# Layer 1 of a four-layer kernel: projections of split operands in three passes, a scan that works in place in three pairs of banks, and sums carried into the next round

## The chip, the core and the metric

The kernel runs on one core of a Trainium2 chip, in one launch. The metric is the device time of one execution in microseconds (us). Five engines run side by side and meet only at semaphores: PE (matrix products; "PEld" is its loading of weights), DVE (vector), ACT (scalar and table functions), POOL (general) and SP (issues most DMAs). PE writes to PSUM, eight banks of 512 fp32 values per partition; DVE and ACT read and write PSUM and SBUF; POOL here works on SBUF.

## What is computed

Four layers run one after the other on x of shape (8, 100, 512): a latent attention with an MLP, this case's layer 1, a cross attention with an MLP, and a grouped attention. Layer 1 is of the RWKV kind (the shift and the norms are cut here):

```
sx = shift(xa) - xa ;  t = tanh((xa + sx*maa_x) @ maa_w1)          # 5 groups of 32
xw, xk, xv, xr, xg = xa + sx*(maa_f + t_f @ maa_w2[f])               # the mixing
w = exp(-exp(time_decay + tanh(xw @ decay_w1) @ decay_w2))
r, k, v = xr @ Wr.T, xk @ Wk.T, xv @ Wv.T ;  g = silu(xg @ Wg.T)
def step(s, inp):                                                     # 32 heads of 16, over the 100 tokens
    a = k_l[..., :, None] * v_l[..., None, :]
    out = einsum('bhs,bhst->bht', r_l, faaaa * a + s)
    return a + w_l[..., None] * s, out
```

## The kernel before, in words

Features lie on the partitions: 512 features are KT = 4 tiles of 128, and the 800 columns of a tile are 8 batches of 100 tokens, cut into two halves of 400. Each stage is a block in which every engine runs its own written list; a barrier stands between blocks. Two stages matter.

`layer1_mixing` computes five branches f = w, k, v, r, g. For each, PE makes eight "mix" tiles (`project_features`, L1259), DVE turns each into sx*(maa_f + mix) (L1445), POOL adds xa (L1458, semaphore `completed`). The branch w then goes through two small decay products (`decay1`, `decay2`, with Tanh and twice Exp on ACT, L1394 to L1405). The other four are multiplied by a weight: PE transposes its 16 blocks (`turn_weight`, L1237), ACT and DVE copy them to SBUF (`copy_weight`), and PE multiplies in fp32 (L1259, `out_f`), ACT copying the results out (L1410). An fp32 matmul shows as two matmul rows in the trace. PE's order is mix_w, turn Wk, mix_k, decay, turn Wv, mix_v, out_k, turn Wr, mix_r, out_v, and so on: a weight is turned before the projection ahead of it. All of it moves through eight PSUM banks in rotation (`Tiles`): a tile waits until the tile eight before it is emptied.

`layer1_scan` goes through the four tiles in four rounds (a loop, m) of 16 steps t. For each step PE spreads row t of v of each head over the head's 16 partitions (a product with `spread[t]`, in the two parts `v.hi` and `v.lo` of a rounded fp32r value and its rest, L1597) into one PSUM pair `ps_v`; DVE multiplies by k into `ps_kv`, of which there are two pairs (L1551); ACT puts the starting state in column 0 of each batch (L1579); DVE runs the recurrence over 8 x 101 columns (`tensor_tensor_scan`, L1561); POOL multiplies by r (L1523), and four steps later (GATHER) PE adds it up in `ps_y` with `gather[t]` (L1607). DVE's order is product t, scan t-1, product t+1, scan t. PE's spreading of t waits for DVE's product t-1, which reads `ps_v`; DVE's product t waits for that spreading and for scan t-2. The last four sums of a round stand in PE's list ahead of the next round's first spreading, and ACT's copy of y (L1582) ends the round.

Lines that the prediction uses: the scan's two loops, and the one place where DVE's product waits:

```
dve.wait_ge(spreaded, at(m, N1, t))
dve.wait_ge(scanned, at(m, N1, t - 2))
```

`at(m, N1, t)` is the semaphore's count when event t of round m has happened.

Of the kernel before, what the change touches and what calls it, by code (L numbers as in the profile page):

```python
# [1262 lines left out]

def layer1_mixing(nc, k, ins, ctx, xa, T):

    with ExitStack() as own:
# [8 lines left out]
        mixed = [sb(f"mixed{i}", [P, KT, B * L]) for i in range(2)]  # L1275
# [8 lines left out]
        natural = [sb(f"W_natural{i}", [P, KT, D]) for i in range(2)]  # L1284
        turned = [sb(f"W_turned{i}", [P, KT, D]) for i in range(2)]
        stages = [("t", 4, "a")]
        for n in range(len(BRANCHES) + 1):
            if 1 <= n < len(BRANCHES):
                stages.append((f"W{BRANCHES[n]}", KT, "ad"))
            if n < len(BRANCHES):  # L1290
                stages.append((f"mix_{BRANCHES[n]}", 2 * KT, "d"))
            if n == 1:
                stages += [("decay1", HALVES, "a"), ("decay2", 2 * KT, "a")]
            elif n:
                stages.append((f"out_{BRANCHES[n - 1]}", 2 * KT, "a"))
        tiles = Tiles(k, "l1m", psum_banks(nc, own, "l1m_ps", 8), stages)
# [7 lines left out]
        completed = sem("l1m_completed")  # L1304
        exped = sem("l1m_exped")
# [3 lines left out]
        def _(sp):  # L1309
# [7 lines left out]
            for n, f in enumerate(BRANCHES[1:]):  # L1317
                if n >= 2:

                    tiles.wait_out(sp, f"W{BRANCHES[n - 1]}")  # L1320
                sp.dma_start(natural[n % 2][:], ins[f"L1_xattn_W{f}"].rearrange("(m p) i -> p m i", p=P)
                             ).then_inc(W_loaded[f], 16)

        @block.tensor
        def _(pe):
            pe.wait_ge(small, 16)

            for half in range(HALVES):
                for part in range(2):
                    j = 2 * half + part  # L1330
                    tiles.wait_free(pe, "t", j)
                    for t in range(KT):
                        if j == 0:
# [4 lines left out]
                                       half_tokens(mixed[0], t, half), start=(t == 0), stop=(t == KT - 1))  # L1338
                    mm.then_inc(tiles.filled, 1)
            def mix(n):  # L1340
                f = BRANCHES[n]
                if n:
                    turn_weight(pe, k, tiles, f"W{f}", natural[(n - 1) % 2], lambda: pe.wait_ge(W_loaded[f], 16))
                else:
                    tiles.wait_out(pe, "t")
                    pe.wait_ge(w2_loaded, 16 * 5)
# [7 lines left out]
            def project(n):  # L1354
                f, m_in = BRANCHES[n], mixed[(n + 1) % 2]
                pe.wait_ge(completed, 2 * KT * (n + 1))
                if f == "w":
                    pe.wait_ge(decay_loaded, 16 * 2)
                    for half in range(HALVES):
                        tiles.wait_free(pe, "decay1", half)  # L1360
                        for t in range(KT):
                            mm = pe.matmul(tiles.bank("decay1", half)[0:L_DECAY, 0:HALF], dw1[:, t, :],
                                           half_tokens(m_in, t, half), start=(t == 0), stop=(t == KT - 1))
# [4 lines left out]
                else:  # L1368
                    tiles.wait_out(pe, f"W{f}")
                    project_features(pe, tiles, f"out_{f}", lambda t, m: turned[(n - 1) % 2][:, t, m * P:(m + 1) * P],  # L1370
                                     lambda t, half: half_tokens(m_in, t, half), KT)

            for n in range(len(BRANCHES) + 1):
                if n < len(BRANCHES):
                    mix(n)
                if n:
                    project(n - 1)

        @block.scalar
        def _(act):  # L1380
            for half in range(HALVES):
                for part in range(2):
# [5 lines left out]
                                   ).then_inc(tiles.emptied["a"], 1)  # L1388
            def finish(n):
                f = BRANCHES[n]  # L1390
                if f == "w":
                    for half in range(HALVES):
# [3 lines left out]
                                       ).then_inc(tiles.emptied["a"], 1)  # L1396
                    for j in range(2 * KT):
# [15 lines left out]
            for n in range(1, len(BRANCHES) + 1):  # L1413
                if n < len(BRANCHES):
                    copy_weight(tiles, "a", act, f"W{BRANCHES[n]}", turned[(n - 1) % 2])
                finish(n - 1)

        @block.vector
        def _(dve):
# [5 lines left out]
            for t in range(KT):  # L1425
                dve.wait_ge(differed, t + 1)
                dve.scalar_tensor_tensor(by_batch(mixed[0][:, t, :]), by_batch(sx[:, t, :]),
                                         column(k, "L1_xattn_maa_x", t), xa[:, t, :, 1:PREV], ALU.mult, ALU.add
                                         ).then_inc(first_mixed, 1)
            for n, f in enumerate(BRANCHES):  # L1430
                if f != "w":
                    copy_weight(tiles, "d", dve, f"W{f}", turned[(n - 1) % 2])
                if n == 1:

                    tiles.wait_out(dve, "t")
                for j in range(2 * KT):
                    m, half = divmod(j, HALVES)
                    tiles.wait_filled(dve, f"mix_{f}", j)
                    if n >= 2 and j == 0:

                        back = BRANCHES[n - 2]
                        tiles.wait_filled(dve, "decay1" if back == "w" else f"out_{back}",
                                          (HALVES if back == "w" else 2 * KT) - 1)

                    dve.scalar_tensor_tensor(half_tokens(mixed[(n + 1) % 2], m, half),  # L1445
                                             tiles.bank(f"mix_{f}", j)[:, 0:HALF], column(k, f"L1_xattn_maa_{f}", m),
                                             half_tokens(sx, m, half), ALU.add, ALU.mult
                                             ).then_inc(tiles.emptied["d"], 1)

        @block.gpsimd  # L1450
        def _(pool):
            k.sems.clear_ended(pool)
            for n, f in enumerate(BRANCHES):
                for j in range(2 * KT):
                    m, half = divmod(j, HALVES)
                    tiles.wait_out(pool, f"mix_{f}", [j])
                    dst = by_batch(half_tokens(mixed[(n + 1) % 2], m, half))
# [3 lines left out]
def layer1_scan(nc, k, ins, ctx, T, yT, prefetch):  # L1461
# [6 lines left out]
    GATHER = 4  # L1468
    with ExitStack() as own:
# [10 lines left out]
        v = Split(own, nc, "v_split", [P, KT, B * L])  # L1480
# [5 lines left out]
        ps_v = own.enter_context(nc.psum_tensor("ps_v", [P, HALVES, 512], F32))  # L1486
        ps_kv = [own.enter_context(nc.psum_tensor(f"ps_kv{i}", [P, 1024], F32)) for i in range(2)]
# [4 lines left out]
        built = sem("l1s_built")  # L1492
        spreaded = sem("l1s_spread")
# [8 lines left out]
        v_split = sem("l1s_v_split")  # L1502
        block = own.enter_context(nc.Block())
# [10 lines left out]
        def _(pool):  # L1514
            k.sems.clear_ended(pool)
            pool.sem_inc(received, 2 * N1)
# [10 lines left out]
        def _(dve):  # L1527
# [5 lines left out]
            dve.tensor_reduce(k.head_of[:], ident, AX.X, ALU.add)  # L1533
            dve.memset(gather[:], 0.0).then_inc(built, 1)
# [3 lines left out]
            dve.wait_ge(built, 2)  # L1538
            for t in range(N1):
                dve.tensor_scalar(spread[:, t, :], k.same_head[:], rows[:, t:t + 1], None, ALU.mult)  # L1540
                last = dve.tensor_copy(gather[:, t, t:P:N1], k.same_head[:, t:P:N1])
            last.then_inc(built, 1)
            for t in range(KT):
                dve.wait_ge(v_rounded, t + 1)
                v.rest(dve, lambda x: x[:, t, :], T["v"][:, t, :]).then_inc(v_split, 1)
            with dve.Fori(0, KT) as m:
                for t in range(N1 + 1):
                    if t < N1:
                        dve.wait_ge(spreaded, at(m, N1, t))
                        dve.wait_ge(scanned, at(m, N1, t - 2))  # L1550
                        dve.tensor_tensor(  # L1551
                            kv[t % 2][:, :, 1:PREV].rearrange("p (h b) l -> p h b l", h=HALVES),
                            ps_v[:, :, 0:HALF].rearrange("p h (b l) -> p h b l", l=L),
                            T["k"][:, bass.ds(m, 1), :].squeeze(1).rearrange("p (h b l) -> p h b l", h=HALVES, l=L),
# [1972 lines left out]
```

## Time and profile before

| | us |
|---|---|
| three runs: median (lowest to highest) | 3405.37 (3399.28 to 3408.23) |
| the profiled execution, its own time | 3410.99 |
| its span, first to last instruction | 3408.9 |
| mixing stage of layer 1, 599.7 to 749.6 | 149.9 |
| scan stage of layer 1, 749.6 to 970.6 | 221.0 |
| PE busy over the whole span | 3079.6 (90%) |
| mean granted PE clock | 0.948 |

The stages follow one another, so what is changed in layer 1 is read from its two stages. In the rows below, times count from the span's start. A duration is that of one instruction with its fixed part; where instructions follow closely, the distance of their starts tells what one costs. "PEclk" is the clock that PE was granted as a share of 2.4 GHz.

### The profile page before, as it was taken

How to read it: one execution, taken by the hardware profiler on the slowest of the kernel's cores; microseconds unless marked ns; L12 is line 12 of the kernel's file. 1: busy time of each engine (PE TensorE's matmuls, PEld its weight loads, DVE VectorE, ACT ScalarE, POOL GpSimd, SP SyncE). 2: the span in 40 equal slices, each digit the busy share in tenths (PEclk: the TensorE clock that was granted, in tenths of full speed). 3: DMA queues.
4: the chain of work that ended last, by engine and by line, in shares of the span. 5: the costliest groups of instructions: out<-in, count | busy, mean ns of one | idle time of the engine just before them, and what ended most of it. 6: DMA issues, size and time to landing. Idle time of an engine off the chain costs nothing. (4 is left out here: it accounts for less than half of the span.)

```text
span 3408.9 us, 47898 instructions
## 1 busy us (share of the span) xinstructions
PE 3079.6 (90%) x17313; PEld 2567.3 (75%) x17313; DVE 1912.0 (56%) x3919; ACT 1470.1 (43%) x3387; POOL 863.1 (25%) x880
## 2 busy tenths in 40 slices
PE   5999898987778789999999988999999997989997
PEld 4777497544434589989999888998989986955663
DVE  2444533328863466665566666666566555147774
ACT  2444442220011244455544644446554464246771
POOL 0222400305541321132011431104101041055632
PEclk9999999988898899999999999999999998988997
DMA  4131020100001320114101241012401023021110
GB/s 125 65 98 40 26 75 6 56 16 0 0 0 37 98 80 27 46 53 130 52 27 46 71 145 45 28 45 76 132 27 53 20 82 102 1 75 39 58 23 20
DMA packets 131964, 182.75 MB, mean 54 GB/s; under 512 B 17743, under 2 KB 99548, under 8 KB 131740
## 3 DMA queue, kind: packets, MB, share of 16 engines
q1 hardware_dynamic: 119012, 143.96, 13.7%
q0 software_dynamic: 12544, 35.77, 3.4%
q8 instruction: 139, 2.28, 0.3%
q14 instruction: 85, 0.70, 0.1%
q10 hardware_dynamic: 184, 0.05, 0.0%
HBM read 165.88 MB, written 13.86 MB: 53 GB/s over the span
## 5 line engine op out<-in xcount | busy, mean ns | idle before, releaser
L71 PE MATMUL l2a<-l_arena,l_arena 128*128 128x400 f32 (+2 forms) x1856 | 652.1, 351 | 34.5 <-DVE l_arena L2724 14.7
L72 PE MATMUL l2a<-l_arena,l_arena 128*128 128x400 f32 (+2 forms) x1856 | 632.7, 341 | 0.0
L73 PE MATMUL l2a<-l_arena,l_arena 128*128 128x400 f32 (+2 forms) x1856 | 632.6, 341 | 0.0
L71 PEld LDWEIGHTS l2a<-l_arena,l_arena 128*128 128x128 f32 (+1 forms) x1856 | 352.4, 190 | 56.8 <-issue 47.0
L72 PEld LDWEIGHTS l2a<-l_arena,l_arena 128*128 128x128 f32 (+1 forms) x1856 | 354.0, 191 | 2.7
L73 PEld LDWEIGHTS l2a<-l_arena,l_arena 128*128 128x128 f32 (+1 forms) x1856 | 352.6, 190 | 2.0
L2589 ACT ACTIVATE l_arena<-l2a 121x384 fp32r<-121x384 f32 (+1 forms) x208 | 99.6, 479 | 442.5 <-PE l2a L2364 442.5
L2384 PE MATMUL l2a<-l_arena,l_arena 121*128 121x384 f32 (+1 forms) x768 | 279.4, 364 | 3.2 <-DVE l_arena L2790 3.2
L2386 PE MATMUL l2a<-l_arena,l_arena 121*128 121x384 f32 (+1 forms) x768 | 264.0, 344 | 0.0
L2385 PE MATMUL l2a<-l_arena,l_arena 121*128 121x384 f32 (+1 forms) x768 | 263.3, 343 | 0.0
L2239 POOL DMA_DIRECT2D p_dram_layer<-l_arena x128 | 62.7, 495 | 726.1 <-DVE l_arena L2790 724.4
L2768 DVE TENSOR_REDUCE neg_max_layer<-l2a 128x1 f32<-128x362 f32 (+1 forms) x208 | 110.8, 533 | 203.0 <-PE l2a L73 196.0
L3337 ACT ACTIVATE probs<-probs,neg_max 100x363 f32<-100x363 f32 x256 | 151.4, 595 | 92.6 <-DVE neg_max L3374 88.8
L3374 DVE CUSTOM_DVE_ANT_0 probs<-scores,mask 100x363 f32<-100x363 f32 x256 | 134.0, 532 | 81.5 <-PE scores L3285 76.0
L2813 DVE TENSOR_TENSOR l_arena<-Qp_layer,l_arena 128x400 fp32r<-128x400 f32 x256 | 155.9, 669 | 18.6 <-ACT l_arena L2630 18.0
L432 POOL TENSOR_SCALAR probs<-probs,inverse 100x464 f32<-100x464 f32 x128 | 83.6, 653 | 299.8 <-DVE inverse L636 299.7
L3293 PEld LDWEIGHTS turned<-ident,probs 100*121 100x121 f32 x768 | 127.5, 208 | 39.0 <-ACT probs L3337 25.9
L2756 DVE TENSOR_TENSOR l_arena<-Qp_layer,l_arena 128x512 fp32r<-128x512 f32 (+1 forms) x208 | 139.1, 671 | 29.7 <-ACT l_arena L2548 29.7
L3293 PE MATMUL turned<-ident,probs 100*121 100x100 f32 x768 | 137.0, 292 | 19.9 <-ACT probs L3337 13.3
L1523 POOL TENSOR_TENSOR rs<-r_tile,state 128x800 f32<-128x800 f32 x64 | 111.5, 1742 | 149.1 <-DVE state L1561 149.1
L2384 PEld LDWEIGHTS l2a<-l_arena,l_arena 121*128 121x128 f32 x768 | 144.6, 188 | 6.0 <-DVE l_arena L2790 3.8
L2790 DVE TENSOR_TENSOR l_arena<-l2a,l_arena 121x384 fp32r<-121x384 f32 (+1 forms) x208 | 112.7, 542 | 63.3 <-ACT l_arena L2589 63.3
(427 smaller groups left out, 6918.1 us busy)
## 6 DMA issues: line engine op xcount, KB each, us to landing
l_arena<-in_L_xattn_wq_dram SPq DMA_DIRECT2D x32, 512.0 KB, 3.5
l_arena<-in_L_xattn_wk_dram SPq DMA_DIRECT2D x32, 512.0 KB, 5.0
l_arena<-in_L_xattn_wv_dram SPq DMA_DIRECT2D x32, 512.0 KB, 3.5
l_arena<-in_L_xattn_wo_dram SPq DMA_DIRECT2D x64, 256.0 KB, 2.7
l_arena<-ctxT_hi POOLq DMA_DIRECT2D x16, 724.0 KB, 4.6
l_arena<-ctxT_lo POOLq DMA_DIRECT2D x16, 724.0 KB, 6.1
l0mlp_staged<-in_L_xattn_mlp_w_dram SPq DMA_DIRECT2D x16, 512.0 KB, 4.1
l2mlp_staged<-in_L_xattn_w_fc_dram SPq DMA_DIRECT2D x16, 512.0 KB, 4.2
```

The lines of the kernel that those rows point to most:

```text
L71: pe.matmul(out, cut_a(a.hi), cut_b(b.hi), start=start, stop=False)
L72: pe.matmul(out, cut_a(a.hi), cut_b(b.lo), start=False, stop=False)
L73: return pe.matmul(out, cut_a(a.lo), cut_b(b.hi), start=False, stop=stop)
L2384: pe.matmul(out, c_hi[s][0:T2, n, rows], probsT.hi[0:T2, n, ring], start=(n == 0), stop=False)
L2385: pe.matmul(out, c_hi[s][0:T2, n, rows], probsT.lo[0:T2, n, ring], start=False, stop=False)
L2386: mm = pe.matmul(out, c_lo[s][0:T2, n, rows], probsT.hi[0:T2, n, ring], start=False, stop=(n == NT2 - 1))
L2756: dve.tensor_tensor(Qt[i % 2].lo[:, :, 0:n], Qp[:, :, c, rows], Qt[i % 2].hi[:, :, 0:n].bitcast(F32), ALU.subtract).then_inc(qt_lo, 1)
L2790: dve.tensor_tensor(probsT.lo[0:T2, :, cols], ps_t[i % 2][0:T2, 0:NT2 * P].rearrange("p (n l) -> p n l", l=P)[:, :, 0:n], probsT.hi[0:T2, ...
L2813: dve.tensor_tensor(u[h % 2].lo[:, t, :].rearrange("p (b q) -> p b q", q=L), head_columns(Qp, h)[:, t], u[h % 2].hi[:, t, :].bitcast(F32). ...
L3293: mm = pe.transpose(ps_turned[h % 2][0:T3, j * L:(j + 1) * L], probs[h % PROBS][:, j * T3:(j + 1) * T3], k.ident[0:L, 0:L])
L3337: act.activation(probs[h % PROBS][:], probs[h % PROBS][:], ACT.Exp, bias=neg_max[:, h % H3:h % H3 + 1], scale=-1.0).then_inc(exped, 1)
L3374: dve.tensor_tensor_reduce(probs[h % PROBS][:], ps_scores[h % SCORES][0:L, 0:N3], mask_add[b % 2][:], -1.0, 3e38, ALU.add, ALU.min, neg_ma ...
```

## The change

In the mixing, the four weighted projections use operands split in two fp32r parts, a rounded one (`hi`, written by ACT) and the rest (`lo`, by DVE): three products hi*hi, hi*lo, lo*hi (`product`, L69) take the place of the fp32 one. Whole values now lie in `T["g"]` (in `T["r"]` for branch w). The split needs ACT to round eight half tiles of each branch and DVE to subtract them, three tiles behind its mixing (REST_BEHIND), and ACT to round and DVE to subtract each turned weight in place of the copies. There is one buffer for a loaded weight and one for a turned one, so PE now turns a weight after the projection ahead of it, and SP loads the next weight once the last is turned. In the scan, PE spreads v into the very pair of banks in which DVE multiplies in place and scans, three pairs in turn; v has a zero column per batch, so 808 columns go in pieces of 512 and 296. The last four sums of a round and the copy of y are carried into the next round (the first round sums zeros, y gets one tile more); part of the building of `spread` goes to ACT, that of `gather` and some zeros to POOL.

PE's list at the start of the mixing, up to the first projection, before (names: `t_four` and `t_decay` are tanh results, `W_natural` the loaded weight, `l1m_ps` the banks):

```order
L1259 MATMUL l1m_ps<-t_four,maa_w 128x400 x8
L1237 MATMUL l1m_ps<-ident,W_natural 128x128 x16
L1259 MATMUL l1m_ps<-t_four,maa_w 128x400 x8
L1362 MATMUL l1m_ps<-mixed,decay_w 64x400 x8
L1259 MATMUL l1m_ps<-t_decay,decay_w 128x400 x8
L1237 MATMUL l1m_ps<-ident,W_natural 128x128 x16
L1259 MATMUL l1m_ps<-t_four,maa_w 128x400 x8
L1259 MATMUL l1m_ps<-mixed,W_turned 128x400 x32
```

and now:

```order
L1259 MATMUL l1m_ps<-t_four,maa_w 128x400 x16
L1366 MATMUL l1m_ps<-T_r,decay_w 64x400 x8
L1259 MATMUL l1m_ps<-t_decay,decay_w 128x400 x8
L1237 MATMUL l1m_ps<-ident,W_natural 128x128 x16
L1259 MATMUL l1m_ps<-t_four,maa_w 128x400 x8
L71 MATMUL l1m_ps<-mixed_hi,W_turned_hi 128x400
L72 MATMUL l1m_ps<-mixed_lo,W_turned_hi 128x400
L73 MATMUL l1m_ps<-mixed_hi,W_turned_lo 128x400
```

One turned weight less stands ahead of the first projection, and the weight it needs is turned behind the decay products.

DVE's list at the end of a round of the scan, before:

```order
L1551 TENSOR_TENSOR ps_kv<-ps_v,T_k 128x8x100 [waits l1s_scanned,l1s_spread]
L1561 SCALAR_TENSOR_TENSOR state<-T_w,ps_kv 128x808 [waits l1s_received,l1s_started,l1s_keyed]
L1549 REGISTER_ALU
L1551 TENSOR_TENSOR ps_kv<-ps_v,T_k 128x8x100 [waits l1s_scanned,l1s_spread]
L1561 SCALAR_TENSOR_TENSOR state<-T_w,ps_kv 128x808 [waits l1s_received,l1s_started,l1s_keyed] x2
```

and now:

```order
L1604 TENSOR_TENSOR ps_kv<-ps_kv,T_k 128x8x100 [waits l1s_spread]
L1611 SCALAR_TENSOR_TENSOR state<-T_w,ps_kv 128x808 [waits l1s_received,l1s_started,l1s_keyed]
L1602 REGISTER_ALU
L1604 TENSOR_TENSOR ps_kv<-ps_kv,T_k 128x8x100 [waits l1s_spread]
L1611 SCALAR_TENSOR_TENSOR state<-T_w,ps_kv 128x808 [waits l1s_received,l1s_started,l1s_keyed] x2
```

The order of DVE is the same; the product no longer waits for a scan. That wait is now PE's, ahead of its spreading.

PE's list at the end of a round, before:

```order
L1597 MATMUL ps_v<-v_split_hi,spread 128x400 x2
L1597 MATMUL ps_v<-v_split_lo,spread 128x400 x2
L1607 MATMUL ps_y<-rs,gather 128x400 x8
L1603 REGISTER_ALU
L1607 MATMUL ps_y<-rs,gather 128x400 x2
L1591 REGISTER_ALU
L1591 COMPARE_AND_BRANCH
```

and now:

```order
L1677 MATMUL ps_kv<-v_split_hi,spread 128x512
L1677 MATMUL ps_kv<-v_split_hi,spread 128x296
L1677 MATMUL ps_kv<-v_split_lo,spread 128x512
L1677 MATMUL ps_kv<-v_split_lo,spread 128x296
L1666 MATMUL ps_y<-rs,gather 128x400 x2
L1671 REGISTER_ALU
L1671 COMPARE_AND_BRANCH
L1666 MATMUL ps_y<-rs,gather 128x400 x8
```

The last four sums of a round no longer stand between its last spreading and the branch; the eight behind the branch are those of the last round.

The diff, cut to its core:

```diff
+REST_BEHIND = 3
 def layer1_mixing(nc, k, ins, ctx, xa, T):
+        whole = [T["r"]] + [T["g"]] * (len(BRANCHES) - 1)
+        mixed = [Split(own, nc, f"mixed{i}", [P, KT, B * L]) for i in range(2)]
+        natural = sb("W_natural", [P, KT, D])
+        turned = Split(own, nc, "W_turned", [P, KT, D])
...
         @block.tensor
             for n in range(len(BRANCHES) + 1):
                 if n < len(BRANCHES):
                     mix(n)
                 if n:
                     project(n - 1)
+                if 1 <= n < len(BRANCHES):
+                    turn_weight(pe, k, tiles, f"W{BRANCHES[n]}", natural,
+                                lambda: pe.wait_ge(W_loaded[BRANCHES[n]], 16))
...
         @block.scalar
+            def round_mixed(n, tiles_of):
+                for j in tiles_of:
+                    m, half = divmod(j, HALVES)
+                    act.wait_ge(completed, 2 * KT * n + j + 1)
+                    mixed[n % 2].round(act, lambda x: half_tokens(x, m, half), half_tokens(whole[n], m, half)
+                                       ).then_inc(mix_rounded, 1)
+            def round_weight(n):
+                for t in range(KT):
+                    tiles.wait_filled(act, f"W{BRANCHES[n]}", t)
+                    turned.round(act, lambda x: x[:, t, :], tiles.bank(f"W{BRANCHES[n]}", t)[:]).then_inc(W_rounded, 1)
             def finish(n):
                 if f == "w":
+                    round_mixed(1, range(KT))
...                  # the two Tanh
+                    round_mixed(1, range(KT, 2 * KT))
...                  # the sixteen Exp
                 else:
                     for j in range(2 * KT):
+                        if n + 1 < len(BRANCHES) and j < KT:
+                            round_mixed(n + 1, (2 * j, 2 * j + 1))
...
+            for n in range(len(BRANCHES)):
+                finish(n)
+                if n + 1 < len(BRANCHES):
+                    round_weight(n + 1)
...
 def layer1_scan(nc, k, ins, ctx, T, y_and_one, prefetch):
+    BANKS = [0, 1, 2] * 5 + [1]
+    PIECES = (slice(0, 512), slice(512, B * PREV))
+    def last_in_banks(t):
+        return max(u for u in range(t - N1, t) if BANKS[u % N1] == BANKS[t])
...
         @block.gpsimd
+            pool.memset(gather[:], 0.0).then_inc(blank, 1)
+            for t in range(N1):
+                last = pool.tensor_copy(gather[:, t, t:P:N1], k.same_head[:, t:P:N1])
+            for tile in rs:
+                last = pool.memset(tile[:], 0.0)
...
         @block.vector
-                        dve.wait_ge(scanned, at(m, N1, t - 2))
-                        dve.tensor_tensor(
-                            kv[t % 2][:, :, 1:PREV].rearrange("p (h b) l -> p h b l", h=HALVES),
-                            ps_v[:, :, 0:HALF].rearrange("p h (b l) -> p h b l", l=L),
+                        spread_v = kv[BANKS[t]][:, :, 1:PREV]
+                        dve.tensor_tensor(spread_v, spread_v, by_batch(T["k"][:, bass.ds(m, 1), :].squeeze(1)),
+                                          ALU.mult).then_inc(keyed, 1)
...
         @block.tensor
+            for half in range(HALVES):
+                pe.matmul(ps_y[:, half, 0:HALF], gather[:, 0, :], rs[0][:, half * 4:(half + 1) * 4, :], start=True, stop=False)
             with pe.Fori(0, KT) as m:
+                for t in range(N1):
+                    pe.wait_ge(scanned, at(m, N1, last_in_banks(t)))
+                    for part in (v.hi, v.lo):
+                        flat = part[:].rearrange("p m b l -> p m (b l)")
+                        for piece in PIECES:
+                            mm = pe.matmul(ps_kv[BANKS[t]][:, piece], spread[:, t, :],
+                                           flat[:, bass.ds(m, 1), piece].squeeze(1),
+                                           start=(part is v.hi), stop=(part is v.lo))
+                    mm.then_inc(spreaded, 1)
+                    gather_heads(m, t - GATHER)
+            for t in range(GATHER):
+                gather_heads(KT, t - GATHER)
```

## Rows read from the trace of the kernel before

**Rows 1.** Windows, layer 1's mixing and scan: us, length, busy (instructions), PEclk, DMA, GB/s.
```profile
599.70:749.60 149.90, 147.59 (x464) 81.52 (x464) 33.55 (x51) 34.34 (x64) 36.97 (x40) 0.97 0.08 28
749.60:970.60 221.00, 164.82 (x512) 100.35 (x513) 185.50 (x168) 21.59 (x76) 111.47 (x64) 0.88 0.03 6
```

**Rows 2.** Waits 749 to 971 us: who waited for whom, us in total, times, longest.
```profile
DVE ps_kv L1551 <- PE ps_v L1597: 24.9, 12, 4.4
```

**Rows 3.** Timeline, one settled scan step: start, us, engine, line, out<-in, count [idle, releaser].
```profile
783.98 1.00 DVE L1551 TENSOR_TENSOR ps_kv<-ps_v,T_k 128x800 f32<-128x800 f32 x1
784.89 1.83 DVE L1561 TENSOR_TENSOR_SCAN state<-T_w,ps_kv 128x808 f32<-128x808 f32 x1
...
785.87 1.50 PE L1607 MATMUL ps_y<-rs,gather 128*128 128x400 f32 x4
...
786.82 1.00 DVE L1551 TENSOR_TENSOR ps_kv<-ps_v,T_k 128x800 f32<-128x800 f32 x1
```

**Rows 4.** Timeline of DVE, from the scan's first round to its second.
```profile
807.59 3.56 DVE L1561 TENSOR_TENSOR_SCAN state<-T_w,ps_kv 128x808 f32<-128x808 f32 x2
...
815.59 1.00 DVE L1551 TENSOR_TENSOR ps_kv<-ps_v,T_k 128x800 f32<-128x800 f32 x1 [4.45 <-PE ps_v L1597]
...
817.68 1.00 DVE L1551 TENSOR_TENSOR ps_kv<-ps_v,T_k 128x800 f32<-128x800 f32 x1 [1.09 <-PE ps_v L1597]
```

**Rows 5.** Timeline of PE, mixing.
```profile
619.63 1.91 PE L1237 MATMUL l1m_ps<-ident,W_natural 128*128 128x128 f32 x16
...
674.74 21.66 PE L1259 MATMUL l1m_ps<-mixed,W_turned 128*128 128x400 f32 x64
...
703.64 44.92 PE L1259 MATMUL l1m_ps<-mixed,W_turned 128*128 128x400 f32 x128
```

**Rows 6.** Timeline of PE in layer 2, split products of 400 columns.
```profile
1902.95 0.34 PE L71 MATMUL l2a<-l_arena,l_arena 128*128 128x400 f32 x1
...
1904.40 0.34 PE L73 MATMUL l2a<-l_arena,l_arena 128*128 128x400 f32 x1
```

**Rows 7.** Timeline of POOL, ACT and PE around the decay projections.
```profile
615.85 14.77 POOL L1458 TENSOR_TENSOR mixed<-mixed,xa 128x400 f32<-128x400 f32 x16 [28.39 <-DVE mixed L1445]
...
632.98 1.28 ACT L1402 ACT_TABLE_LOAD   x1
...
634.28 0.59 ACT L1402 ACTIVATE T_w<-l1m_ps,params 128x400 f32<-128x400 f32 x1
...
642.70 1.07 ACT L1245 ACTIVATE W_turned<-l1m_ps 128x512 f32<-128x512 f32 x2
...
646.13 6.21 PE L1259 MATMUL l1m_ps<-mixed,W_turned 128*128 128x400 f32 x18
```

**Rows 8.** DMA issues in the mixing: count, KB each, us from issue to landing.
```profile
W_natural<-in_L_xattn_Wv_dram SPq DMA_DIRECT2D x1, 1024.0 KB, 8.0
```

**Rows 9.** DVE's groups by form: out<-in, shapes, count, busy, mean ns, idle before.
```profile
L58 DVE TENSOR_TENSOR l0mlp_gT_lo<-l0mlp_g,l0mlp_gT_hi 128x400 fp32r<-128x400 f32 x32 | 18.4, 575 | 89.7 <-ACT l0mlp_gT_hi L54 89.7
...
L58 DVE TENSOR_TENSOR l_hT_lo<-l_whole,l_hT_hi 128x400 fp32r<-128x400 f32 x8 | 5.4, 743 | 0.0
```

**Rows 10.** Timeline of PE, its first product of the scan stage.
```profile
761.09 1.03 PE L1597 MATMUL ps_v<-v_split_hi,spread 128*128 x2 [12.52 <-DVE v_split_lo L58]
```

**Rows 11.** POOL's groups by form.
```profile
L3091 POOL MEMSET values<- 121x768 f32 x2 | 1.5, 737 | 154.4 <-POOLq L949 154.4
...
L866 POOL COPY xa<-states 128x32 f32<-128x32 f32 x1 | 0.2, 235 | 0.0
```

**Rows 12.** Windows of PE: us, length, busy (instructions), PEclk, DMA, GB/s.
```profile
774.00:778.00 4.00, 4.00 (x9) 0.50 0.00 0
...
790.00:806.00 16.00, 12.99 (x46) 1.00 0.00 1
```

**Rows 13.** Timeline of DVE, the first settled product, and the last two scans.
```profile
778.30 1.00 DVE L1551 TENSOR_TENSOR ps_kv<-ps_v,T_k 128x800 f32<-128x800 f32 x1 [1.22 <-PE ps_v L1597]
...
962.32 3.55 DVE L1561 TENSOR_TENSOR_SCAN state<-T_w,ps_kv 128x808 f32<-128x808 f32 x2
```

More of the change, by code:

```diff
@@ L1362, in project @@
                             mm = pe.matmul(tiles.bank("decay1", half)[0:L_DECAY, 0:HALF], dw1[:, t, :],
-                                           half_tokens(m_in, t, half), start=(t == 0), stop=(t == KT - 1))
+                                           half_tokens(whole[0], t, half), start=(t == 0), stop=(t == KT - 1))
                         mm.then_inc(tiles.filled, 1)
@@ L1368, in project @@
                 else:
+                    pe.wait_ge(mix_split, 2 * KT * n)
                     tiles.wait_out(pe, f"W{f}")
-                    project_features(pe, tiles, f"out_{f}", lambda t, m: turned[(n - 1) % 2][:, t, m * P:(m + 1) * P],
-                                     lambda t, half: half_tokens(m_in, t, half), KT)
+                    for j in range(2 * KT):
+                        m, half = divmod(j, HALVES)
+                        tiles.wait_free(pe, f"out_{f}", j)
+                        for t in range(KT):
+                            mm = product(pe, tiles.bank(f"out_{f}", j)[:, 0:HALF], turned, m_in,
+                                         lambda x: x[:, t, m * P:(m + 1) * P], lambda x: half_tokens(x, t, half),
+                                         start=(t == 0), stop=(t == KT - 1))
+                        mm.then_inc(tiles.filled, 1)
             for n in range(len(BRANCHES) + 1):
@@ L1430, in _ @@
             for n, f in enumerate(BRANCHES):
-                if f != "w":
-                    copy_weight(tiles, "d", dve, f"W{f}", turned[(n - 1) % 2])
                 if n == 1:
                     tiles.wait_out(dve, "t")
[L1436 to L1448, printed above, removed]
+                for j in range(2 * KT + (REST_BEHIND if n else 0)):
+                    if j < 2 * KT:
+                        m, half = divmod(j, HALVES)
+                        tiles.wait_filled(dve, f"mix_{f}", j)
+                        dve.scalar_tensor_tensor(half_tokens(whole[n], m, half), tiles.bank(f"mix_{f}", j)[:, 0:HALF],
+                                                 column(k, f"L1_xattn_maa_{f}", m), half_tokens(sx, m, half),
+                                                 ALU.add, ALU.mult).then_inc(tiles.emptied["d"], 1)
+                    if n and j >= REST_BEHIND:
+                        split_mixed(n, j - REST_BEHIND)
@@ L1450, in _ @@
+                if n:
+                    for t in range(KT):
+                        dve.wait_ge(W_rounded, KT * (n - 1) + t + 1)
+                        turned.rest(dve, lambda x: x[:, t, :], tiles.bank(f"W{f}", t)[:]).then_inc(tiles.emptied["d"], 1)
         @block.gpsimd
@@ L1537, in _ @@
                             k.head_of[:].unsqueeze(2).broadcast_to([P, P // N1, N1])).then_inc(built, 1)
[L1538 to L1542, printed above, removed]
             for t in range(KT):
                 dve.wait_ge(v_rounded, t + 1)
-                v.rest(dve, lambda x: x[:, t, :], T["v"][:, t, :]).then_inc(v_split, 1)
+                v.rest(dve, lambda x: x[:, t, :, 1:PREV], by_batch(T["v"][:, t, :])).then_inc(v_split, 1)
+            dve.wait_ge(built, 2)
+            for t in range(0, N1, 2):
+                last = dve.tensor_scalar(spread[:, t, :], k.same_head[:], rows[:, t:t + 1], None, ALU.mult)
+            last.then_inc(spread_dve, 1)
             with dve.Fori(0, KT) as m:
@@ L1587, in _ @@
             pe.sem_inc(spreaded, 2 * N1)
[L1588 to L1589 removed]
+            pe.sem_inc(gathered, 2 * N1 - GATHER)
             pe.wait_ge(v_split, KT)
[L1591 to L1610 removed]
```

132 lines of the change are left out of this document (72 added, 60 removed).

## The prediction

> **What bounds the kernel now.** I read the windows by stage first, since the diff touches two stages of layer 1 only. The mixing takes 149.9 us with PE busy for 147.6 of them: there PE's own work sets the time. The scan takes 221.0 us with PE busy for 164.8, DVE for 185.5 and POOL for 111.5 [rows 1]: nobody fills it. The waits say who is late there: DVE stood 24.9 us before its product, in 12 waits of up to 4.4 us, for PE's spreading of v [rows 2]. The timelines show the two kinds of it. A settled step is 2.84 us from product to product (783.98 to 786.82): the product lasts 1.00, the scan starts 0.91 after it and lasts 1.83, and the next product starts 0.10 after the scan's end [rows 3]. So inside a round DVE is the bound. Between rounds it isn't: the last two scans end at 811.15, the next product starts at 815.59 and the one after it 2.09 later [rows 4], since the next spreading stands behind the last four sums in PE's list and behind DVE's product in turn.
>
> **The mixing.** Four projections of 32 products each, 128 in all. An fp32 product is two rows of the trace; 64 of them take 21.66 us, 0.338 each [rows 5], 0.677 a product. The split form stands in layer 2: from 1902.95 to 1904.40 eight of them start, 0.181 each [rows 6], 0.544 for three. 128 x 0.133 = 17.0 us gained.
>
> Against it stand three losses. First, the path to the first projection. One turned weight (1.9 us [rows 5]) leaves PE's list ahead of the decay products, so these come 1.9 earlier; but ACT must now round four half tiles between the second Tanh and its table load. POOL's adds come every 0.92 (14.77/16); w's are done at 623.2, and k's follow DVE, which puts rests between its products, to about 630.7. The second Tanh ends by 631.1 (632.98 less 1.9), four roundings at no more than 0.535 (two copies of 512 in 1.07) end at 633.2, the table load of 1.28 at 634.5: the first Exp is 0.2 later than 634.28. The sixteen Exps take as long as before, 8.42 (634.28 to 642.70). ACT's four roundings of Wk end at 645.1, DVE's last rest at 646.3, and mix_v's last four tiles need exactly those banks, so PE ends mix_v at 647.0 and starts out_k there, against 646.13 [rows 7]: 0.9 lost. Second, one turned weight more now lies behind that point: 1.9. Third, Wg is turned last, with nothing of PE's behind it: ACT's copy of the last tile and four roundings, then DVE's last rest, end some 4.0 us after out_r, PE's transposes 1.9 after: 2.1 of waiting. Wv and Wr have a mix (5.5 us) to hide in. SP now issues the next weight's load when the last one is turned; the load (8.0 us [rows 8]) has a projection and a mix, 23 us, to hide in, and nothing of this stage stands behind it in SP's queue. The new work of DVE (32 rests of 0.575 [rows 9], and subtractions of weights in place of copies) and of ACT (32 roundings and 8 more of weights) comes to some 20 us each, on top of 33.6 and 34.3 in a stage of 150 [rows 1]; behind out_k it lies beside PE's projections and costs nothing. The dip behind 703.64, where 128 rows take 44.92 and not twice 21.66 [rows 5], follows the same 32-row mix in both and stays.
>
> DVE's rests and POOL's adds both read two tiles of SBUF. A rest of 400 columns takes 0.575 where POOL rests, and 0.743 on average in the one group that ran beside POOL's adds [rows 9]. If the four rests of k held up POOL for their whole length, 4 x 0.575 less the 0.4 of slack (631.1 less 630.7) would be lost, 1.9; by the means of the rows it is 4 x 0.168 less the slack, 0.3. I take 0.5, near the rows, with 0 and 1.9 as ends. The Trainium skill (SBUF — State Buffer, "Who interferes with whom") says that a DVE instruction with two SBUF inputs and a GpSimd one that reads SBUF lock each other out for their whole length. By that rule the loss is the upper end, 1.9, and the mixing's gain 1.4 smaller; the rows agree that they disturb each other, not that each rest does so in full.
>
> Mixing: 17.0 - 0.9 - 1.9 - 2.1 - 0.5 = 11.6 us less.
>
> **The scan's start.** Its first spreading starts at 761.09 [rows 10], 11.5 after the stage [rows 1]. DVE is relieved of zeros, 16 small copies and 8 of its 16 `spread` tiles; POOL takes the zeros and the copies, and new zeros for `rs`. POOL's price by the nearest rows: 768 columns of zeros cost 0.737, a copy of 32 columns 0.235 [rows 11]. 2048 columns are 2.0, 16 copies at most 3.8 (2.4 if they overlap by a third), four times 800 columns 3.1: 7.5 to 9, behind the clearing of semaphores that opens POOL's list and that no row shows; I add 1, and up to 3 more where POOL and DVE disturb each other. PE then starts 11 (8.5 to 13) after the stage. It first sums zeros, four matmul rows at half clock (0.50 [rows 12], so twice 0.338 each), 2.7; the spreading of step 0 takes 1616 columns at 1.2 GHz, 1.35; then come sums of zeros again and the spreading of step 1. If the clock rises behind the first spreading these take 1.35 and 0.73, if it doesn't 2.7 and 1.35; with some 0.4 until DVE starts, the second product stands 17.5 to 19.5 after the stage, and I take 18.1, since PE now works without a break where before it waited until 774. Before, the first settled product, the sixth, stands at 778.30 [rows 13], which puts the second at 17.4 by steps of 2.84. 0.7 lost; with PE's start at 8.5 and a risen clock 2.4 would be gained, at 13 and half clock 4.1 lost.
>
> **The scan's steps.** With three pairs PE spreads up to three steps ahead, and DVE's product no longer waits for the scan before it, which is what left the 0.10 after each scan. Where two DVE instructions follow without such a wait, the second starts before the first ends: the scan 0.09 before the product's end [rows 3], two scans in 3.56 and not 3.66 [rows 4]. So a step becomes 0.91 + 1.73 = 2.64, if the product behind the scan does likewise; the bounds are 2.64 and 2.84. I take 2.64, as both neighbours show it.
>
> Two waits are left in a round. Step 15 shares its pair with step 13, so its spreading starts when scan 13 ends: DVE waits 1.09, as at 817.68 [rows 4], instead of overlapping by 0.10: 1.19. Step 1 of the next round shares with step 15: DVE does product 0 meanwhile (0.91) and stands at 1.09 after the last scan. From product 1 to the end of scan 15: 14 x 2.64 + 1.19 + 0.91 + 3.56 = 42.6; a further round 1.09 + 42.6 = 43.7. Four rounds: 42.6 + 3 x 43.7 = 173.7. Before, from the second product (767.0 by the step above) to 965.87, the end of the last scan [rows 13]: 198.9. Gain 25.2.
>
> What is queued behind the new waits: PE's wait for a scan holds back the sum behind it, which POOL's `rs` buffers of four steps need; POOL (111.5 us over 64 steps, 1.74 each [rows 1]) has them early, since its step is shorter than DVE's. ACT's copy of y, now between steps 3 and 4, delays the column of step 4 by 0.84, which has a step and a half of slack. PE's work of a step is 1616 columns of spreading, 0.73, and four rows of sums, 1.35 by their pace (1.50 with the last one's tail [rows 3]), together 2.08 of 2.64. The tail behind the last scan is unchanged.
>
> Scan: 25.2 - 0.7 = 24.5 less. Together 36.1 less: 3411.0 of the profiled execution become 3374.9. That execution lies 5.6 over the median shown, so against the median 3405.4 it is 3369.
>
> **Rivals.**
> - *No overlap behind the scan.* The step stays at 2.84: four rounds take some 184, the gain of the scan's steps is 14.8, the time 3380. For it: no row shows a product starting behind a scan that it doesn't wait for; against it: both other orders overlap. The Trainium skill (VectorE: DVE Perf Modes, "The DRAIN you can't avoid") says that the next instruction doesn't issue until the pipe is empty, with a semaphore or without; by it this rival would be the forecast. The overlapped starts of [rows 3, 4] speak against it, or make the drain shorter than the rule has it.
> - *In place is slow.* Every DVE row before writes another bank than it reads, or SBUF. If reading and writing one bank take turns, 800 elements cost 0.85 more (1.00 for 800 [rows 3] against 0.575 for 400 [rows 9], twice the difference), 64 times, 54 us: 3423. It decides against the change from 0.56 us a product on. No row excludes it, and none points to it.
> - *PE at half clock.* A step would cost 1.35 + 2.7 = 4.0 on PE, above DVE's 2.64, 64 of them 257 instead of 199: about 3450. Against it: 12.99 busy of 16 us kept the clock at 1.00 [rows 12], and PE's share now is 78% a step without the pauses between rounds.
> - *The mixing pays less.* ACT, POOL and DVE hold up more than I count (1.9 for the locks, the clock after PE's wait for Wg), and the start takes its worst: 1.4, some 1.6 and 3.4 more, 3376.
> - *The start pays*, and no lock costs: 3.6 more gained, 3365.
>
> **How the numbers follow.** The forecast 0.52, with a range of its own from 3361 to 3377; no overlap 0.18; mixing and start worse 0.12; start better 0.08; in place slow 0.07; half clock 0.03. 3357 to 3386 holds the first four and leaves the last two and odd ends out. 0.3%, 10 us, is about what a measurement here can tell. Faster by more: 0.89, the first four less a little; slower 0.08, the last two less a part-priced slow product; within 0.03.
>
> **What would show it.** Split rows at a pace of 0.181 in the mixing and PE waiting about 2 us ahead of out_g; a step of 2.64 with products of 1.00; a wait of about 1.1 at step 15 of each round and none of 4.4; PE's clock at 1.00 from the third step on. A product far over 1.00, a step of 2.84, or a PE that DVE waits for in most steps would make it wrong.

## The result and the profile after

The changed kernel took 3368.4 us (median of four runs, 3366.0 to 3379.6) against 3405.2 for the kernel before beside it (four runs, 3399.3 to 3408.2): a ratio of 0.9901, 95% interval 0.9882 to 0.9919. Two more comparisons, on two different chips, gave 0.9907 (0.9870 to 0.9943) and 0.9905 (0.9888 to 0.9921). 3369 was forecast.

The profiled execution took 3379.6, the slowest of its four; that of the kernel before, 3411.0, lay above all its other runs too. The two spans differ by 31.1 (3408.9 and 3377.8) and the medians by 36.8. The windows of after by stage answer to [rows 1, 12]; below them are a projection, the stretch behind the 32-row mix, the scan's start, and the first spreadings of step 15 in rounds 1 and 4 (columns as there, PEclk third from the end):

```profile
core 0: us, PE busy (x) PEld busy (x) DVE busy (x) ACT busy (x) POOL busy (x), PEclk, DMA share, GB/s
599.53:740.18 140.65, 134.54 (x592) 104.69 (x592) 59.63 (x91) 53.12 (x104) 42.87 (x40) 0.96 0.09 30
740.18:931.87 191.69, 155.62 (x524) 92.59 (x524) 175.01 (x143) 23.65 (x84) 118.89 (x86) 0.95 0.03 7
...
646.94:664.78 17.84, 17.84 (x99) 17.65 (x98) 10.01 (x15) 7.51 (x15) 9.38 (x8) 1.00 0.00 1
697.26:703.00 5.74, 5.74 (x17) 5.69 (x18) 1.09 (x3) 1.35 (x3) 2.77 (x3) 0.50 0.00 0
752.30:754.30 2.00, 2.00 (x7) 1.47 (x6) 0.00 (x0) 0.00 (x0) 0.00 (x0) 0.50 0.00 0
754.30:757.00 2.70, 2.70 (x11) 1.84 (x11) 1.36 (x2) 0.99 (x2) 0.00 (x0) 0.98 0.00 0
793.50:794.60 1.10, 1.05 (x5) 0.94 (x6) 0.01 (x1) 0.00 (x0) 1.02 (x1) 1.00 0.00 0
925.65:927.40 1.75, 1.75 (x5) 1.56 (x6) 0.00 (x1) 0.00 (x0) 1.73 (x1) 0.50 0.00 0
```

The mixing went from 149.9 to 140.65, the scan up to the end of the last scan from 216.3 (749.60 to 965.87, [rows 13]) to 191.69: 9.2 and 24.6, together 33.8. PE, which filled the mixing before, now waits in it. DVE's waits of the scan, answering to [rows 2] (waiter, waited for: us in total, times, longest):

```profile
DVE ps_kv L1604 <- PE ps_kv L1677: 16.6, 9, 8.3
```

8.3 of the 16.6 is the wait ahead of the first product. What is left is in the timeline of DVE: a settled step [rows 3], step 15 and the boundary of the first round [rows 4], and the same of the second:

```profile
775.04 0.97 DVE L1604 TENSOR_TENSOR ps_kv<-ps_kv,T_k 128x800 f32<-128x800 f32 x1
775.92 1.83 DVE L1611 TENSOR_TENSOR_SCAN state<-T_w,ps_kv 128x808 f32<-128x808 f32 x1
777.66 0.97 DVE L1604 TENSOR_TENSOR ps_kv<-ps_kv,T_k 128x800 f32<-128x800 f32 x1
...
794.59 1.00 DVE L1604 TENSOR_TENSOR ps_kv<-ps_kv,T_k 128x800 f32<-128x800 f32 x1 [1.09 <-PE ps_kv L1677]
795.50 3.55 DVE L1611 TENSOR_TENSOR_SCAN state<-T_w,ps_kv 128x808 f32<-128x808 f32 x2
798.97 0.97 DVE L1604 TENSOR_TENSOR ps_kv<-ps_kv,T_k 128x800 f32<-128x800 f32 x1
800.14 1.00 DVE L1604 TENSOR_TENSOR ps_kv<-ps_kv,T_k 128x800 f32<-128x800 f32 x1 [0.20 <-PE ps_kv L1677]
...
838.81 1.00 DVE L1604 TENSOR_TENSOR ps_kv<-ps_kv,T_k 128x800 f32<-128x800 f32 x1 [1.81 <-PE ps_kv L1677]
839.72 3.55 DVE L1611 TENSOR_TENSOR_SCAN state<-T_w,ps_kv 128x808 f32<-128x808 f32 x2
843.19 0.97 DVE L1604 TENSOR_TENSOR ps_kv<-ps_kv,T_k 128x800 f32<-128x800 f32 x1
845.21 1.00 DVE L1604 TENSOR_TENSOR ps_kv<-ps_kv,T_k 128x800 f32<-128x800 f32 x1 [1.04 <-PE ps_kv L1677]
```

A step is 2.62 (775.04 to 777.66), and the product starts at 777.66, 0.09 before the scan's end at 777.75. The boundary of 4.45 and 2.09 is gone. Step 15 waits 1.1 in rounds 1 and 3, but 1.81 in rounds 2 and 4; PE's timeline shows why (behind the 32-row mix and the wait for Wg, answering to [rows 5], then the scan's start and the spreadings of step 15 in rounds 1 and 4):

```profile
691.26 6.00 PE L1259 MATMUL l1m_ps<-t_last,maa_w_last 32*128 32x400 f32 x16
697.19 0.70 PE L71 MATMUL l1m_ps<-mixed_hi,W_turned_hi 128*128 128x400 f32 x1
697.69 0.54 PE L72 MATMUL l1m_ps<-mixed_lo,W_turned_hi 128*128 128x400 f32 x1
...
717.54 1.91 PE L1237 MATMUL l1m_ps<-ident,W_natural 128*128 128x128 f32 x16
721.39 0.42 PE L71 MATMUL l1m_ps<-mixed_hi,W_turned_hi 128*128 128x400 f32 x1 [1.94 <-issue]
...
750.14 3.00 PE L1657 MATMUL ps_y<-rs,gather 128*128 128x400 f32 x4 [11.00 <-POOL rs L1569]
...
793.55 0.63 PE L1677 MATMUL ps_kv<-v_split_hi,spread 128*128 x2 [2.91 <-DVE state L1611]
...
925.65 1.04 PE L1677 MATMUL ps_kv<-v_split_hi,spread 128*128 x2 [2.90 <-DVE state L1611]
```

PE stands 2.9 us for scan 13 in every round. At 793.55 it comes back at a granted clock of 1.00 (2.4 GHz), at 925.65 at 0.50 (1.2 GHz): the same two matmuls take 0.63 and 1.04.

### The profile page after: what moved, and what is told of

Its sections match the earlier page's. It is cut to its first block and busy times, and to the rows that moved or that the text cites. A ratio compares the mean times of both kernels' runs of the same rounds, so it can differ in the third digit from the quotient of the medians.

```text
span 3377.8 us, 48217 instructions
## 1 busy us (share of the span) xinstructions
PE 3059.4 (91%) x17461; PEld 2582.4 (76%) x17461; DVE 1934.5 (57%) x3934; ACT 1493.1 (44%) x3436; POOL 879.2 (26%) x903
## 5 line engine op out<-in xcount | busy, mean ns | idle before, releaser
L2458 PEld LDWEIGHTS l2a<-l_arena,l_arena 121*128 121x128 f32 x768 | 144.5, 188 | 6.0 <-DVE l_arena L2864 3.8
L2459 PEld LDWEIGHTS l2a<-l_arena,l_arena 121*128 121x128 f32 x768 | 145.0, 189 | 2.2
```

The source lines that it names most:

```text
L2458: pe.matmul(out, c_hi[s][0:T2, n, rows], probsT.hi[0:T2, n, ring], start=(n == 0), stop=False)
L2459: pe.matmul(out, c_hi[s][0:T2, n, rows], probsT.lo[0:T2, n, ring], start=False, stop=False)
```

## The experiments

Stage lengths by windows, the scan up to the end of its last scan; the ratio is to the kernel before beside it:

| kernel | mixing | scan | median us | ratio (95%) |
|---|---|---|---|---|
| before | 149.89 | 216.27 | 3405.2 | |
| after, three traces | 140.65, 139.78, 139.80 | 191.69, 191.86, 191.89 | 3368.4, 3373.0, 3368.3 | 0.9901, 0.9907, 0.9905 |
| mixing alone | 139.76 | 215.77 | 3393.4 | 0.9984 (0.9969-0.9999) |
| scan alone | 149.87 | 191.77 | 3380.5 | 0.9945 (0.9926-0.9965) |
| wait for the scan put back | 139.90 | 206.17 | 3388.3 | 0.9960 (0.9943-0.9977) |
| sums kept in the round | 139.58 | 202.30 | 3373.9 | 0.9919 (0.9900-0.9938) |
| pairs in threes throughout | 139.67 | 183.96 | 3370.5 | 0.9885 (0.9851-0.9920) |
| and no sums of zeros | 139.89 | 176.69 | 3355.9 | 0.9856 (0.9822-0.9890) |
| fifth mix over 128 rows | 136.18 | 191.83 | 3364.1 | 0.9883 (0.9846-0.9920) |
| the last three edits together | 136.41 | 176.66 | 3352.4 | 0.9851 (0.9833-0.9870) |

**Each half alone.** The mixing of after with the scan of before, and the other way round.

> Only the mixing is changed; the scan is that of the kernel before. Theory (the two halves of the change are independent, and the mixing pays its measured 9.2 us: 140.65 for the stage in the trace of after, 149.89 in that of before): about 3396, the mixing stage 140 to 141.5, the scan stage 216 to 217 as before. Rival (what the mixing gains is partly handed back behind it, as the 2.9 us by which the trace of after is longer than that of before between the last scan and the end would have it): 3399 or more with a mixing stage of 140.65 all the same.

> Only the scan is changed; the mixing is that of the kernel before. Theory: the scan pays its 24.6 us (191.7 in place of 216.3) whatever stands ahead of it: about 3381, steps of 2.62 to 2.63. Rival (the scan's start, or TensorE's clock in it, hangs on the split products ahead of it): a scan stage 2 us or more away from 191.7. If the theories of this run and of the mixing alone both hold, the two gains come to 33.8 of the 36.8 us of the medians.

Both stages came out as in after (10.1 and 24.5 less than before): the halves are independent. In total time the mixing alone gave 0.3 to 10.5 us by its interval, too wide to tell its theory from its rival. By the medians (before beside them: 3402.8) the two halves gave 9.4 and 22.3.

**Part of the time is not the change's.**

> The changed kernel again, on the chip and beside the runs that the next three are compared with. By the traces so far the mixing stage takes 139.6 to 140.7 and the scan 191.7; what lies behind the last scan, which no edit touches, took from 2437 to 2450 us in six traces, so a single execution is uncertain by that much. Theory: 33 to 37 less than before on the same chip.

It came out 34 less by the medians, 32 by the ratio. From the last scan to layer 2's last product the changed kernel takes 1849.9 us in the profile above and 1850.7 in a third trace of the same kernel; from there to the end, first in the one, then in the other:

```profile
2781.80:3377.80 596.00, 514.03 (x3057) 377.27 (x3056) 336.97 (x947) 293.97 (x576) 211.95 (x144) 0.89 0.15 46
```
```profile
2780.30:3369.40 589.10, 510.58 (x3057) 377.84 (x3056) 333.23 (x947) 293.97 (x576) 212.16 (x144) 0.89 0.15 46
```

596.0 and 589.1: with the same instructions, layer 3 alone differs by 7. So a stage is compared by its own length, and single executions are not. The totals of the next two runs miss what was expected of them by as much, one up and one down (3388 for 3380, 3374 for 3381).

**The wait that went.**

```
 dve.wait_ge(spreaded, at(m, N1, t))
+dve.wait_ge(scanned, at(m, N1, t - 2))
```

> After, with one wait put back: VectorE's product waits for the end of the scan ahead of it in VectorE's own list. Theory (the step fell from 2.84 to 2.63 because that wait is gone, the third pair and in place only make it possible): a settled step of 2.82 to 2.84, 56 steps of 64 by 0.21, so 11.8 us: about 3380. Rival (the product would start 0.09 before the scan's end in any case, since it is VectorE that lets the next instruction in early, and the 0.20 came from PE being ahead): step 2.63, 3368.

DVE's timeline of it, a settled step:

```profile
773.35 1.00 DVE L1605 TENSOR_TENSOR ps_kv<-ps_kv,T_k 128x800 f32<-128x800 f32 x1
774.26 1.83 DVE L1612 TENSOR_TENSOR_SCAN state<-T_w,ps_kv 128x808 f32<-128x808 f32 x1
776.19 1.00 DVE L1605 TENSOR_TENSOR ps_kv<-ps_kv,T_k 128x800 f32<-128x800 f32 x1
```

2.84, the product 0.10 behind the scan's end at 776.09: the step of the kernel before, from this one wait, with three pairs and in place. The rival is refuted. The scan lost 14.5, not 11.8. The settled steps are 52 and not 56, 13 a round, since DVE waits for PE at step 15 either way: 11.2 by 0.215. Step 15 now waited 1.81 in all four rounds and the second product behind each boundary 1.0, in the trace of after only in two rounds and at one boundary: 3.0 more. The rest is the start.

**The sums carried over.**

```
...                                   # ACT's copy of y likewise
-    gather_heads(m, t - GATHER)
-for t in range(GATHER):
-    gather_heads(KT, t - GATHER)
+    if t >= GATHER:
+        gather_heads(m, t - GATHER)
+for t in range(N1 - GATHER, N1):     # inside the round
+    gather_heads(m, t)
```

> After, with the last four sums and the copy of y back at the end of their round, three pairs and in place kept; the first sum of zeros is left out, POOL's zeros are not. Theory (the carrying is what takes away the 4.4 us at each round's end): the last scan is followed by POOL's product, the sums and the next spreading, so VectorE stands about 4.4 us and the product after that 2.1 later, 6.5 in place of 1.1 to 1.9, three times: 15 lost; the start without sums of zeros gains 2 to 3; about 3381. Rival (three pairs alone would do, the next round's spreadings start during the last scans): boundaries of 1 to 2 us, 3366.

The first boundary, DVE's timeline:

```profile
789.52 3.56 DVE L1611 TENSOR_TENSOR_SCAN state<-T_w,ps_kv 128x808 f32<-128x808 f32 x2
797.86 1.90 DVE L1604 TENSOR_TENSOR ps_kv<-ps_kv,T_k 128x800 f32<-128x800 f32 x2 [4.79 <-PE ps_kv L1673]
```

The 4.4 to 4.8 are back, so carrying the sums and the copy is what removed them; but the second product follows the first at once (1.90 for two), since with three pairs PE spreads several steps in a row. The expected 2.1 behind it did not come, and the scan lost 10.6 where 12 to 13 were expected (15 at the boundaries less the start).

**The waits that stayed.** The loop over rounds written out, step t of all 64 in pair t modulo 3:

```
-BANKS = [0, 1, 2] * 5 + [1]
+def pair(m, t):
+    return (N1 * m + t) % 3
-with pe.Fori(0, KT) as m:            # and dve, act, pool
+for m in range(KT):
-pe.wait_ge(scanned, at(m, N1, last_in_banks(t)))
+pe.wait_ge(scanned, at(m, N1, t - 3))
```

> After, with the loop over the four rounds written out, so that the pairs of banks go round in threes over all 64 steps and no two steps two apart share a pair. Theory (step 15's wait of 1.1 to 1.8 and the 1.1 to 1.9 behind each round's last scan come from the shared pair alone, and the larger of each pair of numbers from a spreading at TensorE's half clock after TensorE stood 2.9 us for scan 13): from the second product on DVE has 62 steps of 2.625 without a wait, then 4.44 to the end, 167.2 in place of 175.2: scan stage 183.7, 8 us less than after. Rival (code written out four times has to be fetched, or POOL's product and the sums hold PE at the old places): waits of over 0.5 remain once per 16 steps, gain under 4 us.

DVE's waits in its whole scan:

```profile
DVE ps_kv L1603 <- PE ps_kv L1676: 9.6, 2, 8.2
```

Two waits, ahead of the first two products, and none behind. The scan took 183.96 (183.7 expected), PE's clock was 1.00 from the fourth step to its end. The shared pair made those waits: the loop was written out in the same run, but in the trace of after it is DVE's scan that PE waits for at step 15 (2.91 at 793.55).

**The start.** That, and without the sums of zeros, POOL's zeros for them, and PE's wait for `gather` moved to its first use:

```
-pe.wait_ge(gather_built, 1)
-pe.wait_ge(rs_blank, 1)
-for half in range(HALVES):
-    pe.matmul(ps_y[:, half, 0:HALF], gather[:, 0, :], rs[0][...], start=True, stop=False)
+    if m > 0 or t >= GATHER:
+        gather_heads(m, t - GATHER)
```

> The one before, and the sums of zeros ahead of the first step and in steps 0 to 3 are left out, with POOL's zeros for them. Theory (the first spreading waits for POOL's list, which ends with those zeros at 750.0, 3.7 behind VectorE's and ScalarE's parts, and then for TensorE's sums of zeros at half clock, 2.2): the first product starts 8.5 us after the mixing and not 14.5, the second 10.5 and not 16.5: scan stage 177.5 to 178.5, 6 less than with cyclic pairs alone. Rival (TensorE stays at its lower clock longer without those sums, so that the first steps cost 3.8 in place of 2.6): 2 to 4 of the 6 are lost again.

PE's first spreadings, and DVE's first products:

```profile
746.11 1.01 PE L1668 MATMUL ps_kv<-v_split_hi,spread 128*128 128x512 f32 x2 [7.42 <-DVE spread L1592]
...
751.96 1.04 PE L1668 MATMUL ps_kv<-v_split_hi,spread 128*128 128x512 f32 x2 [1.48 <-DVE state L1606]
```
```profile
747.83 1.00 DVE L1599 TENSOR_TENSOR ps_kv<-ps_kv,T_k 128x800 f32<-128x800 f32 x1 [1.93 <-PE ps_kv L1668]
749.17 1.00 DVE L1599 TENSOR_TENSOR ps_kv<-ps_kv,T_k 128x800 f32<-128x800 f32 x1 [0.35 <-PE ps_kv L1668]
```

The products start 8.1 and 9.4 after the mixing (739.73), 7.3 gained on the kernel above. PE does stay at half clock longer, as the rival has it (1.04 at 751.96), but DVE waits no more behind the second product, so that costs nothing: PE is ahead by then.

**The fifth mix over 128 rows.** `t_last` and `maa_w_last` get 96 rows of zeros.

```
-w2_last = sb("maa_w2_last", [F_MIX, D])
+w2_last = sb("maa_w2_last", [P, D])
-t_last = sb("t_last", [F_MIX, B * L])
+t_last = sb("t_last", [P, B * L])
```

> After, with the fifth mix multiplied over 128 rows, 96 of them zeros, in place of 32. In after the products behind it run at a granted clock of 0.50 for 5.6 us (697.3 to 703.0), which makes that projection 20.35 long and the others 17.84. Theory (it is the 32-row products that make the clock fall): no fall, out_r 17.85, mixing stage 138, 2.5 less. Rival (the clock falls for another reason, such as the turning and mixing by themselves, which before Wv's projection it doesn't): the same fall, mixing 140 to 141.

```profile
687.81 5.54 PE L1259 MATMUL l1m_ps<-t_last,maa_w_last 128*128 128x400 f32 x16
692.88 0.66 PE L71 MATMUL l1m_ps<-mixed_hi,W_turned_hi 128*128 128x400 f32 x1
693.38 0.35 PE L72 MATMUL l1m_ps<-mixed_lo,W_turned_hi 128*128 128x400 f32 x1
```

PE's timeline at the same place: the second product takes 0.35 where it took 0.54, and the clock doesn't fall. The mixing is 3.6 less than in the trace of after beside it, more than the 2.5 expected, because that trace has two falls of the clock and the profile of after only one, a longer one. The second comes 1.0 behind the start of out_g, which PE starts after its wait of 1.94 for Wg. The two falls in the trace of after beside it, then out_g of this run (columns as in [rows 1]):

```profile
695.60:698.80 3.20, 3.20 (x11) 3.20 (x11) 0.76 (x2) 0.00 (x0) 2.88 (x3) 0.50 0.00 0
719.50:722.60 3.10, 3.10 (x11) 3.10 (x11) 0.00 (x0) 0.50 (x1) 0.00 (x0) 0.50 0.00 0
```
```profile
714.55:732.30 17.75, 17.75 (x96) 17.43 (x96) 0.00 (x0) 3.69 (x8) 0.00 (x0) 1.00 0.00 0
```

The padded mix takes both away: out_r takes 17.82 for 19.17, out_g with what follows it in the stage 18.80 for 20.32, the mix 5.07 for 5.57 from start to start; that is 3.4 of the 3.6. Seven traces of the new mixing with the 32-row mix have both falls, the profiled one has the first alone, and the two with the padded mix have none. Why the second goes with the first is not shown.

**All three together.**

> After with the three edits together: pairs of banks going round in threes over all 64 steps, no sums of zeros, the fifth mix over 128 rows. Theory (they lie in stages of their own and add up): mixing 136.2, scan 176.7, so 18.7 less than the 331.6 that the two stages of after took beside these runs: some 19 us less than after, ratio to before 0.984 to 0.986. Rival (the later layers, whose time differs by up to 12 us between executions though nothing in them is changed, swallow part of it): stages as said, ratio above 0.987.

> After beside it, on the same chip: ratio to before 0.989 to 0.992, mixing 139.6 to 140.7, scan 191.7 to 191.9.

The stages add up (313.1 against 331.7). 3352.4 against 3368.3 beside it, ratios of 0.9851 (0.9833 to 0.9870) and 0.9905 (0.9888 to 0.9921), which don't overlap: this version beats the changed kernel too, by 15.9 in the medians and 18.6 in the stages. After beside it came out as expected.

## Why the prediction was right

36.1 was forecast against its own profiled execution; the two stages gave 33.8 to 34.5, the three ratios 32 to 34. The forecast's mechanism held and no rival came whole; but a part of one did, terms of the mixing were off both ways, and two errors in the scan cancelled.

*Mixing: 11.6 forecast, 9.2 to 10.1 measured.* The 9.2 is of the profiled execution, which is not the usual one: the nine other traces with the new mixing agree with one another up to out_k, and the seven of them with the 32-row mix to the end of the stage. Term by term, from the second trace of after (10.1):

- The pace of 0.181 was nearly right (0.183), the 17.0 made of it too large: a projection of 96 rows takes 17.84 and not 17.4, since its second row starts 0.49 behind the first. That is 1.7 over four.
- "The dip ... stays" was right: out_r takes 1.3 more than the others (19.17 for 17.83); before, the dip cost 1.6 [rows 5]. But the sum put at nothing the second fall of the clock, behind PE's wait for Wg: 1.5. The prediction had it among its rivals ("the mixing pays less"), as "the clock after PE's wait for Wg", at 1.6.
- The path to out_k (0.9 and 0.5 forecast) lost next to nothing: out_k starts 46.55 after the stage, before 46.42. ACT's four roundings behind the second Tanh took 1.80 and not 2.14, and DVE's rests beside POOL's adds 0.75 to 0.79, near the mean of the rows (0.743 [rows 9]).
- PE's wait for Wg: 1.94 for 2.1. The weight turned later: 1.9, as forecast.

So 11.6 less 1.7 and 1.5, and 1.3, 0.3 and 0.2 better: 10.2. The profiled execution differs in two places. The first fall lasted 5.7 us there, out_r took 20.35 (697.19 to 717.54) and the mix 6.00 where it otherwise takes 5.64, and no second fall came. And the locks came once: POOL's four adds ran through, and DVE's first rest stood beside them for 2.59 where it needs 0.575 [rows 9]. ACT's last rounding ahead of the table load then waited 0.60 for POOL, and out_k started 1.0 later than before. First DVE, with the same rest in the second trace behind it, then POOL, then ACT:

```profile
624.49 2.59 DVE L58 TENSOR_TENSOR mixed_lo<-T_g,mixed_hi 128x400 fp32r<-128x400 f32 x1 [1.63 <-ACT mixed_hi L54]
```
```profile
623.65 0.75 DVE L58 TENSOR_TENSOR mixed_lo<-T_g,mixed_hi 128x400 fp32r<-128x400 f32 x1 [1.61 <-ACT mixed_hi L54]
```
```profile
622.93 3.72 POOL L1491 TENSOR_TENSOR T_g<-T_g,xa 128x400 f32<-128x400 f32 x4
```
```profile
632.81 0.54 ACT L54 ACTIVATE mixed_hi<-T_g 128x400 fp32r<-128x400 f32 x1 [0.60 <-POOL T_g L1491]
```

The Trainium skill's rule (SBUF — State Buffer, "Who interferes with whom"), by which a DVE instruction with two SBUF inputs contends with a GpSimd one that reads SBUF, fits this one rest, which ended 0.4 after POOL's four adds. Its upper end of 1.9 came in no trace.

*Scan: 24.5 forecast, 24.4 to 24.6 measured.*

- Start: the second product stands 16.5 after the mixing (756.64), 18.1 forecast. POOL was the last, as forecast; PE started at 10.0 and not 11, its clock rose behind the first spreading, as chosen, and the second product came 6.5 behind PE's start and not 7.1. 1.6 better.
- Step: 2.62 for 2.64, 56 times: 0.8 better. The wait put back shows the cause as the prediction put it: 0.215 a step. The Trainium skill (VectorE: DVE Perf Modes, "The DRAIN you can't avoid") found no cost of a semaphore behind each of eight copies; here a wait for the instruction just ahead did cost. The same section says that a next instruction that is not held starts earlier, and the 0.09 in every settled step agrees; so, read whole, it does not forecast the rival of no overlap.
- Waits: 1.09 at step 15 and 1.09 behind the last scan were right for rounds at full clock only. The prediction asked about the clock for a settled step and not for the 2.9 us in which PE stands for scan 13. In the profiled execution the lower clock behind that pause cost 0.72 + 0.85 + 0.72 = 2.3 in rounds 2 and 4 (1.81 for 1.09 twice, and 845.21 for a product that would stand at 844.36). Start and step paid for it. In the other two traces of after it cost 2.1, at step 15 of three rounds.
- In place costs nothing: 1.00 alone, 0.97 behind a scan. PE at half clock throughout: not seen.

The range for the unknowns was sound; that the sum came within one us of the median is partly luck, by the cancelling above and by layer 3's 7 us.

## What to carry over

A wait on one's own engine's last instruction is not free even when it is met: look for the 0.1 behind it and the 0.1 of overlap that it forbids, and buy it off with another buffer. A rotation of buffers must also close at the loop's end; where the count doesn't divide, price the shared step, and ask what clock the engine that stands there comes back with. A sum is to be held against more than one trace: the profiled execution was the odd one of ten. Zeros fed through a pipeline to keep a loop uniform cost their whole length at its start.

## What was not expected of the hardware

- Behind sixteen products over 32 rows, 5.6 us in which PE was never idle, the granted clock was 0.50 for 3.3 us (5.7 in the profiled execution, where it fell within them). It was so in the kernel before too, for 3.4 us [rows 5]. In seven of eight traces of the new mixing with that mix it fell once more, for about as long, some 1 us after PE had come back from its wait for Wg. The same products over 128 rows, 96 of them zeros, kept the clock at full speed in both places, and were faster themselves (5.07 from start to start in place of 5.57).
- The same pause of 2.9 us of PE ended at 2.4 GHz in two rounds and at 1.2 GHz in the other two (in the second and third trace of the same kernel: one and three).
